# A two-layer graph network on one core: another order of the work in its first stage

## The reference

```python
def _lightgcn_layer(x, src, dst, num_nodes):          # used three times
    summed = segment_sum(x[src], dst); counts = segment_sum(ones, dst)
    return summed / maximum(counts, 1.0)[:, None]
x = layernorm(x + L0(x))                              # L0: three such layers
x = layernorm(x + L1(x, edge_attr_2, edge_index))     # L1: two MLPs per node and edge, segment_sum(flux, dst)
```

## Time and profile before

| | us |
|---|---|
| runs | 7063.24, 7046.56, 7058.39 |
| median | 7058.39 |
| profiled execution, its time | 7057.93 |
| profiled execution, its span | 7056.2 |
| GpSimd, TensorE, VectorE busy in the span | 5129.2, 5421.4, 4825.1 |

### The profile page before, as it was taken

The page is one execution under the profiler, slowest core; times in us unless marked ns, Lnnn a source line. Parts: engine busy times, 40 slices in busy tenths (PEclk is TensorE's granted clock), DMA queues, the critical chain, the costliest instruction groups (busy, mean ns, idle before and its releaser), DMA issues.

```text
span 7056.2 us, 174992 instructions
## 1 busy us (share of the span) xinstructions
PE 5421.4 (77%) x50131; PEld 4387.8 (62%) x50131; DVE 4825.1 (68%) x9614; ACT 2676.1 (38%) x5487; POOL 5129.2 (73%) x5000
## 2 busy tenths in 40 slices
PE   2799999999999999946666666666666666666665
PEld 2699999999999999934444444444444444444443
DVE  5899898933223555566777777777777777777776
ACT  2688888820000111123333333333333333333333
POOL 4688887847775777367777777777777777777774
PEclk5899999999999999978888888888888888888888
DMA  6343333356665777656666666666666666666664
GB/s 172 134 140 138 121 139 139 139 183 228 225 226 210 242 236 246 209 149 162 172 175 170 175 174 176 170 174 171 178 170 175 170 177 170 175 171 177 171 175 121
DMA packets 595166, 1239.61 MB, mean 176 GB/s; under 512 B 341448, under 2 KB 434572, under 8 KB 567802
## 3 DMA queue, kind: packets, MB, share of 16 engines
q0 software_dynamic: 209248, 607.84, 32.6%
q1 hardware_dynamic: 330051, 580.86, 25.0%
q10 hardware_dynamic: 55111, 42.41, 2.2%
HBM read 1020.98 MB, written 197.73 MB: 173 GB/s over the span
## 4 chain that ended last, share of the span: by engine, by line
POOL 13%; issue 11%; DMA 11%; PE 6%; ACTq 6%; SPq 5%; ACT 3%; DVE 1%; POOLq 0%; DVEq 0%
POOL edge_rows L2070 13%; DMA edge_rows<-node_table,edge_et 6%; DMA node_sums<-edge_seg 4%; ACTq L1907 4%; PE edge_mp L2098 3%; SPq L1907 3%; ACT edge_h L2174 2%; ACTq L1900 2%; PE edge_tp L2087 1%; PE edge_zp L2109 1%; ACTq L1920 1%; SPq L1900 1%; PE edge_tp L2090 1%; DMA edge_et<-edges_turned 1%; ACT edge_sq L2181 1%
## 5 line engine op out<-in xcount | busy, mean ns | idle before, releaser
L2070 POOL DMA_INDIRECT edge_rows<-node_table,edge_et x3152 | 3003.7, 953 | 961.9 <-issue 920.0
L2087 PE MATMUL edge_tp<-ident,edge_yc 128*128 128x128 f32 x1612 | 529.6, 349 | 1271.3 <-ACT edge_h L2174 1230.5
L1433 PE MATMUL two_acc<-x_parts,win 128*128 128x192 bf16 x16072 | 1386.1, 247 | 17.1 <-issue 11.0
L921 POOL DMA_INDIRECT two_rows<-x_parts,src_at x1120 | 1062.9, 949 | 449.6 <-issue 339.8
L1433 PEld LDWEIGHTS two_acc<-x_parts,win 128*128 128x128 fp8e4 x16072 | 1342.9, 98 | 28.4 <-issue 18.1
L2098 PE MATMUL edge_mp<-edge_h,edge_W 128*128 128x512 f32 x1612 | 1155.4, 850 | 70.1 <-ACT edge_h L2174 68.9
L2166 ACT ACTIVATE edge_yc<-edge_rows 128x512 f32<-128x512 f32 x403 | 253.9, 630 | 2370.8 <-DMA edge_rows<-node_table,edge_et 1839.1
L2087 PEld LDWEIGHTS edge_tp<-ident,edge_yc 128*128 128x128 f32 x1612 | 279.7, 174 | 1362.3 <-issue 1286.5
L1153 ACT ACTIVATE win<-one_count 128x784 fp8e4<-128x784 f32 x1312 | 1070.0, 825 | 147.0 <-PE one_count L1104 82.6
L921 POOL DMA_INDIRECT one_rows<-x_parts,src_at x560 | 864.4, 1544 | 185.2 <-issue 169.4
L1079 PE MATMUL one_acc<-x_parts,win 128*128 128x192 bf16 x8036 | 857.8, 245 | 0.5 <-ACT win L1153 0.5
(11 more groups left out here) (333 smaller groups left out, 7562.5 us busy)
## 6 DMA issues: line engine op xcount, KB each, us to landing
win<-adjacency SPq DMA_DIRECT2D x80, 3136.0 KB
adjacency<-win SPq DMA_DIRECT2D x41, 3136.0 KB
edge_lone_rows<-node_table SPq DMA_DIRECT2D x6400, 1.3 KB
edge_near<-near_ids SPq DMA_DIRECT2D x101, 768.0 KB
edge_rows<-node_table,edge_et POOLq DMA_INDIRECT x3152
edge_act_rows<-node_table ACTq DMA_DIRECT2D x2816, 1.3 KB
two_rows<-x_parts,src_at POOLq DMA_INDIRECT x1120
node_table<-two_row SPq DMA_DIRECT2D x49, 322.0 KB
```

Of the source, the lines that this page charges most:

```text
L921: pool.indirect_dma_start(rows[:, b % ring, e, :], None, XP.rearrange("p (j c) -> (p j) c", c=3 * C), bass.IndirectOffsetOnAxis(ap=src_at[ ...
L1433: mm = pe.matmul(acc[b][:, half * 3 * C:(half + 1) * 3 * C], win[:, b, half, j, :].bitcast(FP8), now[:, j, :], start=(j == 0), stop=(j == ...
L2070: pool.indirect_dma_start(rows[:, h.b, t, :], None, T5, bass.IndirectOffsetOnAxis(ap=et[:, h.b, 0, t:t + 1].bitcast(I32), axis=0))\
L2087: pe.matmul(to, yc[:, h.b % 2, 2 * pr:2 * pr + 2, :].rearrange("p t c -> p (t c)"), ident[:, :], is_transpose=True, start=True, stop=False)
```

## The change

The number of `xp` buffers goes from two to four. The first id of all eight stretches per row is loaded by a DMA of its own from HBM into `first_dst8`, three DMAs on ScalarE's queue ahead of the stage's other loads; `bases()` and `gaps()` are done once, within the search at g = 1. The bfloat16 ids are stored right behind their casts. ScalarE interleaves x parts, edges and turns; `load(2)` and `load(3)` are issued together. VectorE interleaves x parts with `alike(1)` to `alike(3)` and puts `alike(4)` to `alike(6)` between lanes and the wait for `placed`. TensorE turns chunks 0 and 1 before placing. GpSimd clears after gather groups 5 and 6.

```diff
-        xp = sb("xp", [P, 2, JG, 3 * C], BF16)
+        xp = sb("xp", [P, XR, JG, 3 * C], BF16)
+        first_dst8 = sb("first_dst8", [RR, 8], I32)
...
+                if g >= NG - 2:
+                    clear(g - NG + 2)          # GpSimd, in the loop over the gathers
-            clear(0)
             pool.wait_ge(slots_listed, 1)
...                                             # picked gathers
-            clear(1)
...
+            pe.wait_ge(row_used, NG)           # TensorE
+            turns(0)
+            turns(1)
+            for k in range(2):
+                place(k)
+            turns(2)
+            for k in range(2, 4):
+                place(k)
+            turns(3)
+            for k in range(4, NG):
+                place(k)
...
-            act.wait_ge(after_clear, 1)        # ScalarE
+            act.wait_ge(after_clear, 2)
...
+            apart = dst[0:(RR - 1) * ER].rearrange("(r s t) -> r s t", s=8, t=SUB)[:, :, 0:1]
+            act.dma_start(first_dst8[0:RR - 1, :].unsqueeze(2), apart, allow_slow_non_contiguous=True).then_inc(e_after, 16)
...                                             # two more for the last row
-                act.wait_ge(based, k + 1)
+                act.wait_ge(based, 1)
...                                             # at the end of edges(k):
+                act.wait_ge(near_cast, 5 * (k + 1))
+                for r in (slice(0, 96), slice(96, RR)):
+                    act.dma_start(listed[r, :], e_near16[r, :]).then_inc(e_near_out, 16)
...
+            for k in range(2):
+                load(k)
+            edges(0)
+            split_x(0)
+            turns(0)
+            split_x(2)
+            edges(1)
+            split_x(4)
+            turns(1)
+            split_x(6)
+            load(2)
+            load(3)
+            for k in range(2, 4):
+                edges(k)
+                turns(k)
...
+            def bases():                       # VectorE
+
+                dve.wait_ge(e_after, 80)
+                oe.link(dve.tensor_scalar(base[:, :], first_dst8[:, :], float(N - 1), None, ALU.min))
+                oe.link(dve.memset(base[0:1, 0:1], 0.0))
+                dve.tensor_scalar(base_below[:, :], base[:, :], -1.0, None, ALU.mult).then_inc(based, 1)
...                                             # search, after passing(g + 1):
+                if g == 1:
+                    bases()
+                    gaps()
...
-            bases(0)
             split_src()
-            split_x()
+            for k in range(4):
+                split_x(2 * k)
+                if k < 3:
+                    alike(k + 1)
...                                             # loop over g, after lanes_ready:
+                if g < NEAR - 2:
+                    alike(g + 4)
                 dve.wait_ge(placed, g + 1)
...
-                if g < 3:
-                    bases(g + 1)
-                if g == 3:
-                    gaps()
-                if g < NEAR:
-                    alike(g + 1)
-            alike(NEAR + 1)
```

More of the change, by code:

```diff
@@ L520, in find_nodes @@
             sem(n) for n in ("consts", "order", "pool_order", "starts", "ends", "asked", "told", "slots_in", "slots_listed"))
-        x_in, x_out = [sem(f"x_in{b}") for b in range(XR)], [sem(f"x_out{b}") for b in range(2)]
+        x_in, x_out = [sem(f"x_in{b}") for b in range(XR)], [sem(f"x_out{b}") for b in range(XR)]
         x_cast, x_less, x_masked, based, near_cast = (sem(n) for n in ("x_cast", "x_less", "x_masked", "based", "near_cast"))
@@ L560, in _, with clear @@
                                        base=k * P - i, pattern=[[1, P]], channel_multiplier=-2).then_inc(consts, 1)
+            def clear(k):
+                pool.wait_ge(e_turned, 8 * k + 8)
+                pool.memset(e_dst[96:RR, k, :], PAD_DST).then_inc(e_clear, 1)
+                pool.memset(e_src[96:RR, k, :], 0).then_inc(e_clear, 1)
+                pool.memset(e_nv[96:RR, k, :, :], 0.0).then_inc(e_clear, 1)
             pool.wait_ge(dst_written, 32)
@@ L596, in _, with place @@
                 mm.then_inc(row_seen, 1)
-            for k in range(NG):
+            def place(k):
                 pe.wait_ge(lanes_ready, k + 1)
@@ L603, in _, with turns @@
                 mm.then_inc(placed, 1)
-                if k >= 4:
-                    continue
+            def turns(k):
                 pe.wait_ge(near_cast, 5 * (k + 1))
@@ L661, in edges, with split_x, turns @@
                 act.activation(e_src_f[:, :], e_src[:, b, :], ACT.Copy).then_inc(near_cast, 1)
[L663 to L681, removed]
-            split_x()
-            for k in range(4):
+                listed = NEAR16.rearrange("(r t) -> r t", t=ER)[:, k * HE:(k + 1) * HE]
+                act.wait_ge(near_cast, 5 * (k + 1))
+                for r in (slice(0, 96), slice(96, RR)):
+                    act.dma_start(listed[r, :], e_near16[r, :]).then_inc(e_near_out, 16)
+            def split_x(first):
+                part = lambda g, i: xp[:, g % XR, :, i * C:(i + 1) * C]
+                for i in range(3):
+                    for g in range(first, min(first + 2, NG)):
+                        if i == 0:
+                            act.wait_ge(x_in[g % XR], 16 * (g // XR + 1 + (g == NG - 1)))
+                            if g == NG - 1:
+                                act.wait_ge(x_masked, 1)
+                            if g >= XR:
+                                act.wait_ge(x_out[g % XR], 16 * (g // XR))
+                        else:
+                            act.wait_ge(x_less, less_at(g, i - 1))
+                        act.activation(part(g, i), x0[:, g % XR, :, :], ACT.Copy).then_inc(x_cast, 1)
+            def turns(k):
                 b = k % 2
-                if k:
-                    edges(k)
                 if k >= 2:
@@ L731, in _ @@
                 sp.dma_start(XP[:, g * JG * 3 * C:(g + 1) * JG * 3 * C],
-                             xp[:, g % 2, :, :].rearrange("p j c -> p (j c)")).then_inc(x_out[g % 2], 16)
+                             xp[:, g % XR, :, :].rearrange("p j c -> p (j c)")).then_inc(x_out[g % XR], 16)
                 if g + XR < NG:
                     load(g + XR)
-            for b in range(2):
-                sp.wait_ge(x_out[b], 16 * len(range(b, NG, 2)))
+            for b in range(XR):
+                sp.wait_ge(x_out[b], 16 * len(range(b, NG, XR)))
             sp.wait_ge(src_out, 16)
@@ L749, in _ @@
             dve.memset(after[:, :], N - 1).then_inc(after_clear, 1)
+            dve.memset(first_dst8[:, :], N - 1).then_inc(after_clear, 1)
             dve.memset(wide[:, :], 0.0)
@@ L752, in _, with split_x @@
             o.link(dve.tensor_scalar(real[:, :], node_id[:, J - 1:J], float(N), None, ALU.is_lt))
-            def split_x():
+            def split_x(first):
                 def mask():
@@ L759, in mask @@
                     dve.tensor_scalar(x0[:, g % XR, JG - 1, :], x0[:, g % XR, JG - 1, :], real[:, 0:1], None, ALU.mult).then_inc(x_masked, 1)
[L761 to L768, removed]
+                if first == NG - 1:
+                    mask()
+                for i in range(2):
+                    for g in range(first, min(first + 2, NG)):
+                        dve.wait_ge(x_cast, cast_at(g, i))
+                        own = x0[:, g % XR, :, :]
+                        dve.tensor_tensor(own, own, xp[:, g % XR, :, i * C:(i + 1) * C], ALU.subtract).then_inc(x_less, 1)
             def split_src():
@@ L781, in _ @@
             oe = Chain(dve, e_order)
[L783 to L791, removed]
+            def bases():
[3 more added lines that the diff above has]
+                dve.tensor_scalar(base_below[:, :], base[:, :], -1.0, None, ALU.mult).then_inc(based, 1)
             def alike(d):
@@ L807, in gaps @@
             def gaps():
-                dve.wait_ge(e_after, 32)
                 oe.link(dve.tensor_tensor(gap[:, 0:7], base[:, 1:8], base[:, 0:7], ALU.subtract))
```

16 lines of the change are left out of this document (4 added, 12 removed).

## The result

The changed kernel takes 7016.42 us, the median of six runs (7013.20 to 7024.04), against 7051.54 for six of the kernel before (7046.56 to 7063.24): 35 us less, a ratio of 0.9949 with a 95% interval of 0.9936 to 0.9962. A later comparison, five runs against nine, gave 0.9948 (0.9934 to 0.9961). The forecast was 26 us less, 7032, with faster at 0.82; the range (7008 to 7048) holds the time. Of the 16 us between 7032 and 7016, 7 lie in the kernel before, whose median is 7051.54 over six runs and was 7058.39 over the three that the forecast started from; 9 are a larger gain.

A forecast was written before the change was run, and what follows sets the result against it. VectorE's chain in find_nodes waits, no engine being full; its end moves from 209.6 to 182.5 us, 27 us, less 1 for passes meeting worse: 7057.9 - 26 = 7031.9, about 7032. Range 7008 to 7048.

The forecast's parts named there:

- Bases inside the search: Before the split, bases and gaps add 1.1 us plus a 1.2 us wait for new loads (bounds zero and 20).
- ScalarE becomes the chain, the buffers save nothing by themselves: Interleaved x parts, edges and turns on ScalarE: VectorE's last subtraction ends at 101.4 us, 4 us later than before.
- Gathers held up by the passes: GpSimd's gathers beside VectorE's alike passes take some 4.4 us each; the 42nd ends at about 112 instead of 92.5.
- The clearings: GpSimd behind the 42nd gather: clear(0) ends at 118 us, seven more gathers at 128, clear(1) at 132.
- the second clearing: Sign in the new trace: its memsets at 125 to 137 us, ScalarE's loads of chunk 3 right behind.
- What is late next: Load of chunk 3 waits for clear(1), edges(2) behind it; group 2's copies done at 147.0, VectorE waits 20 us.
- From there to the end: VectorE's chain after group 2's copies at 147.0: groups 3 to 6, turns(3), place(4) and tail, ending at 182.5 us.
- Costs set at nothing: New loads' issue, early turns of chunks 0 and 1, ids' store and span loads on SyncE cost no time.
- the longest wait: Sign in the new trace: VectorE's longest wait is 15 to 25 us, before the copy of group 2.
- the tail's end: Sign in the new trace: VectorE's tail, where find_nodes ends, finishes at 178 to 190 us.
- the first rival: Gathers aren't held up by VectorE's passes: tail end 162.7, a gain of 47 us, 7011; chance 0.13 for 7004 to 7018.

The follow-up runs named there:

- the version with more room: Changed kernel with clear(0) behind gather group 4, clear(1) within group 5, turns(3) in two halves, bases and gaps at g = 2; stage end 162.0 us, median 7014.07 us.

## Why the prediction was right, and where its size was off

1. *Bases inside the search:* right. The wait was 1.09 us for the 1.2 written, and the split began at 52.77 for 52.5. What the single numbers cost more was on ScalarE's queue, idle there: the issue of the eight bases per row took 0.94 us, that of the last row's behind it 2.15. 806 numbers are asked for, and over the whole execution ScalarE's queue (q10 in the profile) carries 55,933 packets for 55,111, 822 more, with the same 42.41 MB. That agrees with the rule that the forecast took from the Trainium skill ("DMA: Bandwidth & Descriptors", rules for kernel authors); but the wait stayed near the lower bound and not, as it was read there, the upper.
2. *ScalarE becomes the chain, the buffers save nothing by themselves:* right in the new order. The last subtraction ended at 101.25 for 101.4, and the run with two buffers has it at 102.2. In the old order they save 5.5 us.
3. *Gathers held up by the passes:* the mechanism was right, and this is the term that was mis-sized. The 42nd gather ended at 103.94 and not at 112; against before (92.5) it came 11.5 us later, not 19.5 (whose parts, as written, add up to 19.2). Of the 11.5, 9.8 are `alike(1)` to `alike(3)`. Two things were off. I let one gather through an `alike` pair, from the row at 50.19, where two passes with one input held a gather to the end of the second. Beside an `alike` pair the gather ends 0.8 us after the first pass, while the second still runs, and the next is held by what is left of the second:

```profile
79.11 3.52 DVE L830 TENSOR_TENSOR find_same<-src_f 128x3232 bf16<-128x3232 f32 x1
79.31 4.14 POOL L573 DMA_INDIRECT find_near<-dst_padded,find_near_idx  x1 [0.30 <-issue]
82.67 1.84 DVE L832 TENSOR_TENSOR find_same<-find_same 128x3232 bf16<-128x3232 bf16 x1
83.75 1.57 POOL L573 DMA_INDIRECT find_near<-dst_padded,find_near_idx  x1 [0.30 <-issue]
```

   So a pair costs 3.2 + 0.6 us, not 4.4, and the third, whose gather came 1.2 us into the first pass, 2.2 + 0.6. And with the gathers sooner, the 42nd was through before `alike(4)` began (104.42), which I had counted in with 4.4; of the lanes, set at 3, one operation lay before it and held it 0.6 us.
4. *The clearings:* 2 us too much in the first. Its memsets ran beside the first pass of `alike(4)` without loss, 0.95 and 1.80 us as alone:

```profile
104.42 3.52 DVE L830 TENSOR_TENSOR find_same<-src_f 128x3232 bf16<-128x3232 f32 x1
...
105.76 1.80 POOL L567 MEMSET nv_buf<- 5x2048 f32 x1
```

   But the seven gathers behind it took 12.0 us and not 10: the second pass of `alike(4)` and the pair of `alike(5)`, which I had beside the clearing, lay among them (gathers of 1.56, 3.18 and 1.57 us). The two errors cancel by luck, so what is left is in the main step 3: the second clearing ended at 123.3, for 132.
5. *What is late next:* right, and shown by two runs. The wait at group 2 was 10.1 us, for 20. Of the difference 8.7 us are those of steps 3 and 4; from the clearing's end to the copies' end it took 14.2 us for 15.0, and VectorE was ready 0.6 us later than forecast. Taking the clearing forward gave 7.4 us, taking the held gathers away 11.5.
6. *From there to the end:* right. From the end of the copies of group 2 (137.55) to 172.65 is 35.1 us, for 35.5 (147.0 to 182.5).
7. *Costs set at nothing:* the store of the ids was wrong. I had `edges(3)` off the path. In the new order its casts end at 140.14, only 2.4 us before TensorE reaches turns(3) at 142.54, and the late store makes them 8.7 us later (145.33 for 136.63): that part of the change carries 6.4 us, 4.6 of them here. The forecast of the whole wasn't touched, since it was made for the store as it now is. The span loads were hidden, as said; in the version with more room they are no longer.

The terms add up to the 37.0 us of the stage: 27.1 forecast, 10.1 us less of waiting at group 2, less 0.6 for VectorE ready later, plus 0.4 in step 6. That the time came 35 us down on the median and not 26 is therefore in the main one term, the hold on the 42nd gather in step 3: 11.5 us and not 19.5. By it three of the signs that the forecast named were missed: the second clearing (119.7 to 123.3 for 125 to 137), the longest wait (10.1 for 15 to 25) and the tail's end (172.65 for 178 to 190). Of the first rival (gathers not held up, 7011) the time is near, but its mechanism didn't happen: the gathers took 4.13, 4.14 and 3.13 us.

The rule of the Trainium skill on the shared ports ("SBUF — State Buffer", SBUF: two separate sides) adds that an operation with two SBUF inputs blocks GpSimd only where that reads SBUF. The unhurt memsets in step 4 agree with it. That the lock keeps the other engine out for the whole instruction agrees with the gathers of 3.99, 4.13 and 4.14 us, none of which ended before the pass beside which it began; that a gather could end within the second pass isn't told by it. And length alone does not hold a gather: beside the reduction of `alike(6)`, 3.52 us with one input, three took 0.94 to 0.95 us.

```profile
123.15 3.52 DVE L823 TENSOR_REDUCE find_hits<-find_same 128x32 f32<-128x3232 bf16 x1 [0.15 <-DVE find_lane_start L878]
...
124.73 0.94 POOL L582 DMA_INDIRECT picked<-src_split,slot_at  x1 [0.30 <-issue]
```

One reading fits every gather named here, though no run tests it by itself. Beside a pass with two inputs only the first 0.1 us or so of a gather has to wait, and then its other 0.8 us run beside VectorE's next pass (a second one of two inputs, or a reduction). Beside the splits, its end has to wait too: the gather from 52.43 began before the split at 52.77 and still ended only 0.1 us after it.

```profile
52.43 2.30 POOL L573 DMA_INDIRECT find_near<-dst_padded,find_near_idx  x1 [0.30 <-issue]
```

What stays open is how the 37 us divide: the parts don't add. Undoing the passes' places, the ids' store and the buffers one at a time takes 8.7, 6.4 and 0.9 us from it; bases and buffers alone give -2.2 and 5.5. The rest may need bases early and the new order of ScalarE and TensorE together (turns of chunks 0 and 1 ahead of the lanes); that pair wasn't run by itself, so this is not shown.

## What to carry to other kernels

A wait that the profile shows can be worth nothing if another, for a chain that runs beside, ends right behind it: follow both chains to the place where they meet before pricing one. When work is moved into an engine's idle time, price what it does to the engine that it can hold up, and what is queued behind that one: here passes put into free time cost some 11 us through a clearing and a load at the head of another queue, and the new places of all six passes are worth 8.7 us even so. In a queue in order, a load that must wait costs all that stands behind it, however ready that is.

## What the runs showed of the hardware

- How a gather of GpSimd (0.94 us alone) is held depends on VectorE's operation. Begun beside one split pass with another right behind it (1.84 and 2.00 us), it ended 0.1 us after the second (3.99 us); begun 0.3 us ahead of a split pass, 0.1 us after that one (2.30 us). Beside a pass of two inputs it ended some 0.8 us after that pass, whatever came next (4.13, 4.14 us). Beside a reduction of 3.52 us it wasn't held (0.94 us).
- Memsets of GpSimd (0.95 and 1.80 us) and a float32 pass of two inputs ran side by side, both at their usual length.
- 800 loads of a single number and six more for the last row had all landed 9.3 us after the first were asked for and 6.1 us after the last, beside loads of 448 KB for x; VectorE went on with the last of them, so when the 800 landed isn't told. Their issue took 0.94 us, three times that of a plain load, and the whole made 822 packets.
